# Softmax sums of an attention block: thirteen slots of a group go directly through TensorE instead of eighteen

## What is computed

```
q, k, v = split(x @ w_qkv)                      # 16 heads of 32
q, k = unit_norm(q), unit_norm(k)               # then rotary embedding on the even heads
logits = einsum('bshd,bthd->bhst', q, k) * q_gain[None, :, None, None]
logits = where(causal, logits, lowest)
attn = softmax(logits, axis=-1)
y = einsum('bhst,bthd->bshd', attn, v).reshape(B, S, Dm)
x = layernorm(x + y @ w_out)
```

## Time and profile before

| | us |
|---|---|
| median of 3 runs | 1271.09 |
| lowest and highest | 1271.07 and 1278.27 |
| the profiled execution | 1259.98 |
| its span, first to last instruction | 1258.2 |
| TensorE matmul busy | 1135.2 |
| VectorE busy | 626.7 |
| ScalarE busy | 544.3 |
| GpSimd busy | 520.8 |

### The profile page before, as it was taken

One profiled execution on the slowest core, in us unless ns is written; L12 is line 12 of the kernel. 1 busy time (PEld: TensorE's weight loads), 2 busy tenths in 40 slices (PEclk: granted clock), 3 DMA queues, 4 the chain that ended last, 5 costly groups with the idle time before them and its releaser, 6 DMA issues.

```text
span 1258.2 us, 19860 instructions
## 1 busy us (share of the span) xinstructions
PE 1135.2 (90%) x6618; PEld 805.7 (64%) x6619; DVE 626.7 (50%) x1120; ACT 544.3 (43%) x894; POOL 520.8 (41%) x376
## 2 busy tenths in 40 slices
PE   5559899998988989998988997998999999998986
PEld 5436355653555535565336886777999999996764
DVE  2424776367661676645755845532222222225775
ACT  2226666566654666556763531111332322221212
POOL 1002454136440364413683303665346464606630
PEclk9769999999988999899998988999999999998988
DMA  5952412334132241323605400655344444316541
GB/s 143 367 151 67 119 34 84 95 91 117 37 88 71 85 117 41 85 68 105 181 1 178 147 1 34 219 201 170 96 140 151 148 145 143 124 48 185 157 136 67
DMA packets 92925, 145.93 MB, mean 116 GB/s; under 512 B 12528, under 2 KB 37104, under 8 KB 92848
## 3 DMA queue, kind: packets, MB, share of 16 engines
q1 hardware_dynamic: 76624, 107.68, 28.2%
q10 hardware_dynamic: 10944, 19.93, 4.6%
q0 software_dynamic: 5280, 17.31, 4.2%
HBM read 86.68 MB, written 58.20 MB: 115 GB/s over the span
## 4 chain that ended last, share of the span: by engine, by line
PE 66%; DVE 15%; issue 6%; POOL 5%; DMA 3%; ACT 3%; SPq 1%; POOLq 0%; ACTq 0%; DVEq 0%
PE scores L500 12%; PE bank L1106 10%; PE scores L1138 7%; PE bank L493 7%; PE scores L557 6%; PE bank L1163 6%; PE bank L595 5%; PE scores L417 3%; PE bank L1160 3%; POOL key_sum L1465 3%; ACT probs L1264 2%; PE scores L515 1%; PE bank L1120 1%; DMA turn_scratch<-turned_l 1%; DVE x L833 1%
## 5 line engine op out<-in xcount | busy, mean ns | idle before, releaser
L1264 ACT ACTIVATE probs<-scores,shift_now 128x1024 f32<-128x1024 f32 (+3 forms) x320 | 299.0, 985 | 132.6 <-PE scores L1138 65.3
L1138 PE MATMUL scores<-q_stack,k_stack 96*128 96x512 f32 (+3 forms) x640 | 205.6, 425 | 21.6 <-DMA k_stack<-turn_scratch 12.8
L1138 PEld LDWEIGHTS scores<-q_stack,k_stack 96*128 96x128 f32 x640 | 116.0, 198 | 156.5 <-issue 76.1
L1465 POOL TENSOR_TENSOR key_sum<-key_sum,probs 128x512 f32<-128x512 f32 (+2 forms) x76 | 154.4, 2032 | 128.9 <-ACT probs L1264 125.2
L1379 DVE TENSOR_TENSOR key_sum<-key_sum,probs 128x1536 f32<-128x1536 f32 (+2 forms) x76 | 157.6, 2074 | 43.7 <-ACT probs L1264 41.8
L1163 PE MATMUL bank<-probs,v_sb 128*32 128x512 f32 (+3 forms) x1280 | 154.6, 556 | 0.0
L500 PE MATMUL scores<-ffn_w,xt_h 128*128 x624 | 131.9, 334 | 4.8 <-issue 4.7
L936 POOL TENSOR_TENSOR ffn_w<-raw,ones 128x1408 fp32r<-128x1408 f32 (+2 forms) x36 | 71.8, 2006 | 147.7 <-PE bank L493 103.5
L500 PEld LDWEIGHTS scores<-ffn_w,xt_h 128*128 128x128 f32 x624 | 103.2, 191 | 14.0 <-issue 11.9
L557 PE MATMUL scores<-x1T_h,ffn_w 128*128 128x512 f32 (+1 forms) x384 | 101.5, 402 | 0.7 <-DVE silu L800 0.7
L940 POOL TENSOR_TENSOR ffn_w<-raw,ffn_w 128x1408 fp32r<-128x1408 f32 (+2 forms) x36 | 91.0, 2539 | 2.1
(11 more groups left out here) (208 smaller groups left out, 1858.8 us busy)
## 6 DMA issues: line engine op xcount, KB each, us to landing
q_stack<-turn_scratch SPq DMA_DIRECT2D x48, 256.0 KB, 3.9
k_stack<-turn_scratch SPq DMA_DIRECT2D x48, 256.0 KB, 3.9
x_sorted<-zeros SPq DMA_DIRECT2D x1, 9984.0 KB, 29.2
y_sorted<-y_tile ACTq DMA_DIRECT2D x39, 256.0 KB, 2.3
x_tile<-x_sorted ACTq DMA_DIRECT2D x37, 256.0 KB, 2.7
turn_scratch<-turned_h SPq DMA_DIRECT2D x32, 256.0 KB, 2.6
turn_scratch<-turned_l SPq DMA_DIRECT2D x32, 256.0 KB, 3.4
raw<-w_gate SPq DMA_DIRECT2D x8, 704.0 KB, 5.4
```

The lines of the kernel that those rows point to most:

```text
L1138: mm = nc.tensor.matmul(scores[:, p, hh, lo:CH], k_stack[0:3 * HD, h, j * P:(j + 1) * P], q_stack[0:3 * HD, i % 2, h, lo:CH], start=True, ...
L1264: nc.scalar.activation(probs[:, slot % 4, 2 * p:2 * p + 2, lo:CH], scores[:, p, :, lo:CH], ACT.Exp, bias=shift_now[:, p:p + 1]).then_inc(e ...
L1465: nc.gpsimd.tensor_tensor(key_sum[:, 3, lo:CH], key_sum[:, 3, lo:CH], new, ALU.add).then_inc(sum_pool, 1)
```

## The change

The table of direct slots changes, and nothing else. Slots 10, 14, 15, 28, 29, 36 and 38 leave it and are added on VectorE and GpSimd; slots 13 and 31 enter it. Slots 10 and 38 are 256 wide, the others full. Of 40 slots 13 are direct, not 18.

```
-DIRECT = set(range(STEP_AT[1])) | {4, 5, 6, 10, 11, 14, 15, 23, 28, 29, 30, 36, 38, 39}
+DIRECT = set(range(STEP_AT[1])) | {4, 5, 6, 11, 13, 23, 30, 31, 39}
```

## The result

| | before | change |
|---|---|---|
| median of the runs, us | 1274.65 (4 runs) | 1318.22 (4 runs, 1315.28 to 1326.78) |
| ratio, 95% interval | | 1.0353 [1.0288, 1.0418] |
| span of the profiled execution | 1258.2 | 1318.4 |
| first exponentials to first L417 in that execution | 77.0 to 666.2 = 589.2 | 76.3 to 707.5 = 631.2 |
| the rest of it, first L417 to the end | 592.0 | 610.9 |

A forecast was written before the change was run, and what follows sets the result against it. VectorE's norm chain, not TensorE, was taken to come last where the turns wait, and to start later. Terms 21.3 + 5.45 + 6.0 - 1.6 + 3 = +34 us on 1271 gave 1305 us, range 1287 to 1318.

The forecast's parts named there:

- Slots 28 to 32: Slot 29's addition delays VectorE's norms: +5.1 us, with 2 for the low clock +7.1 in each of groups 0 to 2.
- Slots 36 to slot 1 of the next group: Slot 36's addition delays the norms: +3.45 us plus 2 for the clock in group 0, +3.0 in groups 1 and 2.
- Slots 10 to 24: TensorE waits some 3.4 us for the read of old sums before slot 13, yet -0.4 us a group, -1.6 in all.
- Group 3: Additions of 28 and 29 queue behind the split (1.5 us), slot 31 direct +0.9, `pe_sums` waiting for 38 +0.6: +3 us.
- my third rival: VectorE and GpSimd as adders become the bound in runs of additions: some 3 us a group more, 1317 us; chance 0.07.
- the term for step 2: Slots 10 to 16, all four groups: first direct slot 13 waits for `sums_read`; -0.4 us a group, -1.6 in all.
- The price of the clock: Half-rate TensorE behind the long waits: 2 us at slot 31 in groups 0 to 2 and slot 38 of group 0.
- (4): Rival: TensorE is the bound everywhere, so only the saved matmuls count, -14 us: 1257 us; chance 0.05.
- (2): Rival: late norms without a price of the clock, no low stretches, step 2 at full clock: 1289 us; chance 0.20.
- (5): Rival: savings and delays cancel, full speed in step 2 and norms delayed by half: about 1276 us; chance 0.06.
- (3): Rival: the pair of adders, VectorE and GpSimd, becomes the bound; some 3 us a group more, 1317 us; chance 0.07.

The follow-up runs named there:

- kept_full: The change plus 60 unused identity transpositions on TensorE ahead of the waits of slots 31 and 38, groups 0 to 2; ratio 1.0231, attention 616.4 us.
- only_28: The kernel before with slot 28 alone added; ratio 1.0019 [0.9990, 1.0049], attention 594.4 us.
- norms_first: The change with VectorE's norms put ahead of the addition in slots that have both (29 and 36); ratio 1.0220, attention 609.0 us.

## Why the prediction was right in kind and short in size

*Slots 28 to 32.* The norm chain late by an addition that waits for exponentials, the savings of slots 28 and 29 lost in the wait, +5.1 without the clock: in kept_full, where the clock has no part, the exponentials move by 5.0 to 5.1 us from slot 29 to slot 33 in each of groups 0 to 2. With the clock, 7.2 to 7.5 us in the change against 7.1 forecast. Right.

*Slots 36 to slot 1 of the next group.* The wait grew from 1.93 to 7.2 as forecast (6.8); the turn moved by 4.4 us, not 3.9, since L1353 did take 0.29 us but L1312 of the same norms took 0.87 instead of 0.18 beside GpSimd's additions. In sum the three groups lost 11.5 us, against 5.45 + 3.0 + 3.0 = 11.45 forecast, but not as forecast: +9.0, -0.6 and +3.1. That the sum agrees is luck. In group 0 the price of the clock was not 2 but about 5 (9.0 us against 4.1 in kept_full), since it stayed low for 13 us and into the next group. In group 1 the low clock was there before, and so was a wait of 3.65 us for the turned q (DMA q_stack<-turn_scratch, scores at 380.15), which is 1.90 us in the change.

*Slots 10 to 24.* I took -0.4 a group from the wait for `sums_read`. The wait is there (3.49 us), and up to slot 17 the net is -0.2, -0.8, -0.9 and -0.4. But at slot 25 the groups 1 to 3 have lost 1.6 us, of which 1.2 to 1.6 are left at slot 28: behind the idle before `pe_sums` of step 2, present before, the clock was low (L1173 at 326.29 took 1.84 us; 1.06 before). Sum +1.7 in place of -1.6. Whether the change brings this is open: only_28, which leaves the place alone, shows the same 1.5 to 1.6 us in three groups, and kept_full, which has the change there, in one.

*Group 3.* +3 forecast; from slot 28 to L417 it was +7.2, and 6.9 in kept_full. From slot 29 to 33 it was +4.7 where I had 1.5 + 0.9: the exponentials of slot 31 waited 3.6 us longer for GpSimd's additions, and the clock was low behind that. I had 0.6 for `pe_sums` waiting for slot 38; it waited 2.30 us and then ran at half rate, +3.2. In this group the pair of adders, my third rival, was the bound, twice.

**The steps that failed** are sizes of terms. Between +34 and the 42 us of the attention are 8 us, and by place they are about +0.8 at slots 29 to 33, nothing in sum at slots 36 to 1, +3.3 at slots 10 to 28, +4.2 in group 3 and -0.5 at slots 1 to 9. The largest is the term for group 3: +3 forecast, +7.2 measured, because I let the adders' queue behind the split cost 1.5 us and `pe_sums` 0.6, and they cost 3.6 and 2.3 with a low clock behind both. The second is the term for step 2: -1.6 forecast, +1.7 measured, by a low clock at `pe_sums` that I had counted nowhere.

The price of the clock was mis-sized as well. I had 2 us at each of four places; kept_full gives 2.1 to 2.4 us at each slot 31, but about 5 at slot 38 of group 0. My upper bound of 3.3 us a place came from single stretches of before, which had no wait of 7 us. The 14.8 us of kept_full can't be set against my 8, though: of them 6.8 are at slots 29 to 33 and 6.1 at slots 36 to 1, where groups 1 and 2 pay for a low clock that before has too, and 1.9 elsewhere. And my range ended at 1318, while the high ends of my own terms, as I wrote, gave 1320.

The rivals: TensorE as the bound everywhere (4) is out, and only_28 shows it directly. (2), no price of the clock, is out by kept_full. That savings and delays cancel (5) is out. The adders (3) are out for groups 0 to 2 by only_28 and norms_first, and have their part in group 3.

## What to carry to other kernels

Before moving work onto an engine that looks idle, look at what stands behind it in that engine's queue. An addition that must wait for its input holds up everything behind it, and 1.8 us of work cost 4.2 us of delay here, one slot earlier nothing in groups 0 to 2. Work saved ahead of a wait is worth nothing, and the idle that it leaves may bring the low clock. Then compare several executions: a single trace of this kernel can differ by some us through the clock alone. Price that clock by a kernel that fills the wait with useless work.

## What the hardware showed that I had not expected

- The low clock (1.2 GHz) came behind waits of 1.9, 3.8 and 7 us, but not always behind 1.9: group 0 of before had 1.00 there, groups 1 and 2 had 0.50. Over all kernels, groups 0 to 2, the 4 us behind the turns of slots 31 and 38 had low clock in 15 of 15 cases with a wait of 5.7 to 7.3 us, in 10 of 12 with 2.6 to 3.9 us, in 12 of 21 with 1.9 us at slot 38, and in none of 18 with 1.1 to 1.3 us at slot 31. At `pe_sums` of step 2, with 1.2 to 1.6 us, it came in 14 of 54, group 3 included. Filling a 7 us wait down to 2.95 us of idle did not keep it up, down to 2.84 in another group it did, and down to 0.35 it did.
- It can outlast the wait: in group 0 of the change, L1173 took 1.94 us instead of 1.06, 9 us after the wait had ended, with TensorE busy in between.
- The Trainium skill (TensorE: Matmul & The Clock Gate, "HAM oscillation — how this bites in real kernels") tells to avoid long idle gaps. The rows here agree for the waits of 5.7 us and more, and show the fall behind 1.89 and 2.95 us too, though not each time.
- An instruction of 128x32 elements on VectorE with two inputs took 1.16 us instead of 0.19 beside a GpSimd addition of 1.31 us. The Trainium skill says that a VectorE instruction with two inputs in SBUF contends with a GpSimd one that reads SBUF (SBUF — State Buffer, "Who interferes with whom"), and these durations agree; on a chain that others wait for, this counts in full.
